# Routing weights of a mixture of experts: spread over partitions by DMA through DRAM, in place of a matmul for each block and half

## The reference

```python
hid = hidden_states + attn_out
x2 = rmsnorm(hid, ln2_w).reshape(-1, h)
probs = softmax(x2 @ gate_w.T)                        # 16 experts
top_w, top_i = top_k(probs, 4)
top_w = top_w / sum(top_w, -1)
wfull = sum(one_hot(top_i, E) * top_w[..., None], 1)  # (1024, 16)
gu = einsum('th,eih->tei', x2, w1)                    # I = 176 rows an expert
act = silu(gu[..., :I]) * gu[..., I:]
down = einsum('tei,ehi->teh', act, w2)
routed = einsum('te,teh->th', wfull, down)
shared = silu(sg) * su @ sh_down_w.T                  # 352 rows
return hid + routed + shared
```

## Time and profile before

| | |
|---|---|
| median of 3 runs | 862.36 us (861.4 to 862.72) |
| time of the profiled execution | 861.11 us |
| its span | 859.4 us |
| mean granted TensorE clock | 0.969 |
| PE, DVE, ACT, POOL busy | 769.5, 635.9, 447.4, 361.4 us |
| DMA | 28.37 MB |

### The profile page before, as it was taken

The page is one execution under the profiler, slowest core; times in us unless marked ns, Lnnn a source line. Parts: engine busy times, 40 slices in busy tenths (PEclk is TensorE's granted clock), DMA queues, the critical chain, the costliest instruction groups (busy, mean ns, idle before and its releaser), DMA issues. The chain is left out here.

```text
span 859.4 us, 12018 instructions
## 1 busy us (share of the span) xinstructions
PE 769.5 (90%) x4058; PEld 566.6 (66%) x4080; DVE 635.9 (74%) x1051; ACT 447.4 (52%) x950; POOL 361.4 (42%) x195
## 2 busy tenths in 40 slices
PE   6972887788877999999999999998689999999996
PEld 2420332334434588898889889987567888787876
DVE  5799999998998888766774776676567463736366
ACT  3557565667656356645672765466444242415141
POOL 9048999978886885111120111111253131313130
PEclk9996999989999999999999999999889999999998
DMA  8000000000000200100000010000121110202001
GB/s 297 11 1 1 0 1 0 0 1 1 0 1 1 99 1 25 50 25 26 26 26 25 24 49 25 19 20 19 55 92 56 37 57 21 71 18 73 18 0 49
DMA packets 10905, 28.37 MB, mean 33 GB/s; under 512 B 1648, under 2 KB 3184, under 8 KB 10736
## 3 DMA queue, kind: packets, MB, share of 16 engines
q1 hardware_dynamic: 10864, 27.86, 9.7%
HBM read 26.80 MB, written 1.05 MB: 32 GB/s over the span
## 5 line engine op out<-in xcount | busy, mean ns | idle before, releaser
L316 POOL TENSOR_TENSOR m_ring<-m_du,m_b_sb 128x1024 f32<-128x1024 f32 x64 | 152.5, 2402 | 26.3 <-ACT m_b_sb L549 23.8
L731 DVE TENSOR_TENSOR_SCAN m_ring<-ps,m_ring 128x1024 f32<-128x1024 f32 x64 | 145.2, 2280 | 3.5 <-ACT ps L581 3.2
L1001 POOL TENSOR_TENSOR a_wl<-raw,a_wh 128x1024 fp32r<-128x1024 f32 x16 | 39.9, 2496 | 233.3 <-ACT a_wh L1198 233.0
L425 PE MATMUL ps<-m_ring,ident 128*128 128x512 f32 x256 | 128.2, 616 | 0.4 <-DVE m_ring L736 0.4
L1489 POOL TENSOR_TENSOR e_wl<-raw,e_wh 128x512 fp32r<-128x512 f32 (+1 forms) x55 | 57.2, 1046 | 164.7 <-ACT e_wh L1605 89.8
L856 PE MATMUL ps<-e_rms_hi,e_wh 128*128 128x512 f32 x200 | 87.0, 435 | 3.6 <-ACT e_sg L1618 3.6
L581 ACT ACTIVATE ps<-m_delta,m_negA 128x510 f32<-128x510 f32 x128 | 82.6, 682 | 6.8 <-DVE ps L724 3.7
L425 PEld LDWEIGHTS ps<-m_ring,ident 128*128 128x128 f32 x256 | 50.9, 199 | 45.8 <-issue 43.1
L858 PE MATMUL ps<-e_rms_hi,e_wl 128*128 128x512 f32 x200 | 79.8, 399 | 0.0
L857 PE MATMUL ps<-e_rms_lo,e_wh 128*128 128x512 f32 x200 | 79.3, 396 | 0.0
L1618 ACT ACTIVATE e_sg<-ps 128x512 f32<-128x512 f32 x50 | 29.4, 589 | 84.3 <-PE ps L858 84.3
(11 more groups left out here) (210 smaller groups left out, 2148.8 us busy)
## 6 DMA issues: line engine op xcount, KB each, us to landing
raw<-in_expert_w SPq DMA_DIRECT2D x30, 384.0 KB, 3.0
raw<-in_attn_w SPq DMA_DIRECT2D x20, 512.0 KB, 3.3
m_first<-in_xT SPq DMA_DIRECT2D x2, 512.0 KB, 5.1
x<-in_x_tok SPq DMA_DIRECT2D x1, 1024.0 KB, 10.5
out<-hid SPq DMA_DIRECT2D x8, 128.0 KB, 2.0
m_first<-in_w_x SPq DMA_DIRECT2D x1, 512.0 KB, 7.2
m_first<-in_w_in SPq DMA_DIRECT2D x1, 512.0 KB, 8.0
raw<-in_w_out SPq DMA_DIRECT2D x1, 512.0 KB, 8.6
```

The lines of the kernel that those rows point to most:

```text
L316: nc.gpsimd.tensor_tensor(split(slot(n)), du[:, pair_of(ph):pair_of(ph) + 2, halves(ph)], b_sb[:, n % B_BUFS:n % B_BUFS + 1, :].to_broadca ...
L425: nc.tensor.matmul(ps[:, Y_BANK + c, :], ident[:, :], slot(n)[:, c * HALF:(c + 1) * HALF], start=False, stop=False, skip_group_check=True) ...
L731: nc.vector.tensor_tensor_scan(slot(n), dA_of(n), slot(n), 0.0, ALU.mult, ALU.add).then_inc(scan_done, 1)
L1001: nc.gpsimd.tensor_tensor(w[1][:, j, :], raw[:, j, :], w[0][:, j, :].bitcast(F32), ALU.subtract).then_inc(w_done, 1)
```

## The change

The weights `wf` are turned as float32 (no split in three), 16 experts on 16 partitions of PSUM banks 6 and 7, copied to `wT` (16 x 1024 float32), and stored by SP to a buffer in DRAM. From there SP loads, for each routed block, a tile `wb[:, k, :]` of 128 partitions by 1024 tokens: each partition gets the 4 KB line of its row's expert, so all partitions of one piece read the same line. A block takes two DMAs, cut where the expert changes, or in the middle. aw then multiplies by `wb` in SBUF. `u_ready` is signalled by the last up matmul. `own`, `wp` and their making fall away. SP's loop is written out; the spreads stand in one queue with the loads: first those of the two routed blocks of group 0 and of blocks 0 to 2 of group 1, then each behind a load.

```diff
@@ attention, POOL
-        nc.gpsimd.memset(own[:], 1.0).then_inc(own_ones, 1)
-        pool.wait_ge(own_ones, 1)
-        for part in range(3):
-            rows = own[NW * part:NW * (part + 1), :, :]
-            for sign, base in ((1, 0), (-1, EI - 1)):
-                nc.gpsimd.affine_select(out=rows, in_=rows, compare_op=ALU.is_ge, fill=0.0, base=base,
-                                        pattern=[[sign * P, NM_R], [sign, P]], channel_multiplier=-sign * EI
-                                        ).then_inc(own_done, 1)
-                pool.wait_ge(own_done, 2 * part + (1 if sign > 0 else 2))
@@ expert_block, SP
+            def load(g, j):
+                sp.wait_ge(w_done, g * GM + (j + 1 - GM))
+                sp.dma_start(raw[:, j, 0:FPACK], d["expert_w"][g * GM + j]).then_inc(ld_w[j], 16)
+
+            def spread(g, k):
+                row = (g * GM + k - SH_TILES) * P
+                cut = min(EI - row % EI, P)
+                cut = P // 2 if cut == P else cut
+                if g > (k < SH_TILES):
+                    sp.wait_ge(aw_done, 2 * ((g - 1) * GM + k + 1))
+                for lo, hi in ((0, cut), (cut, P)):
+                    e = (row + lo) // EI
+                    sp.dma_start(wb[lo:hi, k, :], wt_dram[e:e + 1, :].to_broadcast([hi - lo, T])
+                                 ).then_inc(ld_wb[k], 16)
+
+            for j in range(GM):
+                load(1, j)
+            sp.wait_ge(wT_done, 1)
+            sp.dma_start(wt_dram, wT[:]).then_inc(wt_stored, 16)
+            sp.wait_ge(wt_stored, 16)
+            for k in range(SH_TILES, GM):
+                spread(0, k)
+            for k in range(SH_TILES):
+                spread(1, k)
+            for g in range(2, NMG + 1):
                 for j in range(GM):
-                    sp.wait_ge(w_done, g * GM + (j + 1 - GM))
-                    sp.dma_start(raw[:, j, 0:FPACK], ...).then_inc(ld_w[j], 16)
+                    load(g, j)
+                    if g > 2 or j >= SH_TILES:
+                        spread(g - 1, j)
@@ POOL
-                if k == 0:
-                    nc.gpsimd.memset(wp[:], 0.0).then_inc(wp_clear, 1)
@@ PE, gate_up
-                    if o == 0 or shared:
-                        mm.then_inc(ready, 1)
-                if not shared:
-                    if known and n == N_SH:
-                        pe.wait_ge(wT_done, 1)
-                    pe.wait_ge(aw_done, n - 1)
-                    rows = own[:, bass.ds(g * GM + (k - SH_TILES), 1), :].rearrange("p a n -> p (a n)")
-                    nc.tensor.matmul(ps[:, 4 + th, :], rows, wT[:, toks], start=True, stop=True).then_inc(u_ready, 1)
+                    mm.then_inc(ready, 1)
@@ PE, turn_weights
-                pe.wait_ge(wp_done, 1)
-                turned = ps[:, 6, :].bitcast(BF16)
+                pe.wait_ge(wf_done, 1)
                 for i in range(TT):
-                    mm = nc.tensor.transpose(turned[:, i * P:(i + 1) * P], wp[:, i, :], identb[:])
+                    mm = nc.tensor.transpose(banks(ps, 6, 2)[0:NE, i * P:(i + 1) * P], wf[:, i, :], ident[:])
@@ DVE, routing_weights
-                chain(nc.vector.tensor_copy(wp[:, :, 0:NE], wf[:]))
-                chain(nc.vector.tensor_tensor(wr[:], wf[:], wp[:, :, 0:NE], ALU.subtract))
-                chain(nc.vector.tensor_copy(wp[:, :, NW:NW + NE], wr[:]))
-                chain(nc.vector.tensor_tensor(wr[:], wr[:], wp[:, :, NW:NW + NE], ALU.subtract))
-                nc.vector.tensor_copy(wp[:, :, 2 * NW:2 * NW + NE], wr[:]).then_inc(wp_done, 1)
@@ DVE, products
-                nc.vector.tensor_tensor(aw[:, th, :], sg[:, th, :], ps[:, 4 + th, :], ALU.mult).then_inc(aw_done, 1)
+                if th == 0:
+                    dve.wait_ge(ld_wb[k], g * 32 + 32 if k >= SH_TILES else g * 32)
+                nc.vector.tensor_tensor(aw[:, th, :], sg[:, th, :], wb[:, k, th * HALF:(th + 1) * HALF], ALU.mult
+                                        ).then_inc(aw_done, 1)
@@ DVE, tiles
-                        nc.vector.tensor_copy(wT[:], ps[:, 6, :].bitcast(BF16)).then_inc(wT_done, 1)
+                        nc.vector.tensor_copy(wT[:], banks(ps, 6, 2)[0:NE, :]).then_inc(wT_done, 1)
```

More of the change, by code:

```diff
@@ L41 @@
 NMG = NM // GM
-NW = 32
 FPACK = 3 * D
@@ L934, in attention_block @@
     hid, ident, identb, mask = (keep[k] for k in ("hid", "ident", "identb", "mask"))
-    raw, own = keep["raw"], keep["own"]
+    raw = keep["raw"]
     w, q, k_, v, p, pT, o = space.w, space.q, space.k, space.v, space.p, space.pT, space.o
@@ L940, in attention_block @@
     wh_done, w_done, hid_ready = keep["wh_done"], keep["w_done"], keep["hid_ready"]
-    own_ones, own_done = sem("own_ones"), sem("own_done")
     sq_done, root = keep["sq_done"], keep["root"]
@@ L1429, in split @@
         return sb(f"e_{name}h", shape, F32R), sb(f"e_{name}l", shape, F32R)
-    x1, hid, ident, identb, raw, own, gate_raw = (keep[k] for k in ("x1", "hid", "ident", "identb", "raw", "own", "gate"))
+    x1, hid, ident, raw, gate_raw = (keep[k] for k in ("x1", "hid", "ident", "raw", "gate"))
     ld_w = keep["ld_expert"]
@@ L1439, in expert_block @@
     wf = sb("e_wf", [P, TT, NE])
-    wr = sb("e_wr", [P, TT, NE])
-    wp = sb("e_wp", [P, TT, P], BF16)
-    wT = sb("e_wT", [P, T], BF16)
+    wT = sb("e_wT", [NE, T])
+    wb = sb("e_wb", [P, GM, T])
+    wt_dram = nc.dram_tensor("wt", (NE, T), F32, kind="Internal").ap()
     sg = sb("e_sg", [P, 2, HALF])
@@ L1454, in expert_block @@
     lg_ready, rt, ex_done = sem("lg_ready"), sem("rt"), sem("ex_done")
-    wp_clear, wp_done, wT_ready, wT_done = sem("wp_clear"), sem("wp_done"), sem("wT_ready"), sem("wT_done")
+    wf_done, wT_ready, wT_done, wt_stored = sem("wf_done"), sem("wT_ready"), sem("wT_done"), sem("wt_stored")
+    ld_wb = [sem(f"ld_wb{k}") for k in range(GM)]
     g_ready, u_ready = sem("g_ready"), sem("u_ready")
@@ L1470, in _ @@
         def _(sp):
-            with sp.Fori(1, NMG + 1) as g:
+            def load(g, j):
[21 more added lines that the diff above has]
+            for g in range(2, NMG + 1):
                 for j in range(GM):
-                    sp.wait_ge(w_done, g * GM + (j + 1 - GM))
-                    sp.dma_start(raw[:, j, 0:FPACK], d["expert_w"][bass.ds(g * GM + j, 1)].rearrange(
-                        "a p n -> (a p) n")).then_inc(ld_w[j], 16)
+                    load(g, j)
+                    if g > 2 or j >= SH_TILES:
+                        spread(g - 1, j)
             for i in range(TT):
@@ L1521, in gate_up @@
                 known = isinstance(n, int)
-                shared = known and n < N_SH
                 if th == 0:
@@ L1690, in routing_weights, with products @@
                 chain(nc.vector.reciprocal(tot[:], tot[:]))
-                chain(nc.vector.tensor_tensor(wf[:], ex[:], tot[:].to_broadcast([P, TT, NE]), ALU.mult))
-                dve.wait_ge(wp_clear, 1)
-                chain(nc.vector.tensor_copy(wp[:, :, 0:NE], wf[:]))
-                chain(nc.vector.tensor_tensor(wr[:], wf[:], wp[:, :, 0:NE], ALU.subtract))
-                chain(nc.vector.tensor_copy(wp[:, :, NW:NW + NE], wr[:]))
-                chain(nc.vector.tensor_tensor(wr[:], wr[:], wp[:, :, NW:NW + NE], ALU.subtract))
-                nc.vector.tensor_copy(wp[:, :, 2 * NW:2 * NW + NE], wr[:]).then_inc(wp_done, 1)
-            def products(n, th):
+                nc.vector.tensor_tensor(wf[:], ex[:], tot[:].to_broadcast([P, TT, NE]), ALU.mult).then_inc(wf_done, 1)
+            def products(g, k, th):
+                n = g * (2 * GM) + (2 * k + th)
                 dve.wait_ge(u_ready, n + 1)
@@ L1734, in tiles @@
                         routing_weights()
-                    products(n, 0)
+                    products(g, k, 0)
                     if k == GM - 1:
                         low(n, k, 0)
-                    products(n + 1, 1)
+                    products(g, k, 1)
                     if k < GM - 1:
@@ L1783, in constants @@
     }
-    keep["own"] = keep["rest"][:, 0:NM_R * P // 2].bitcast(BF16).rearrange("p (m n) -> p m n", n=P)
     for name in ("ld_small", "wh_done", "w_done", "hid_ready", "x_kept", "sq_done", "root"):
```

## The result

The changed kernel takes **853.78 us** (median of 4 runs, 853.27 to 855.35); the kernel before, on the same chip, 862.54 (861.4 to 863.75). The ratio is 0.9893, with a 95% interval of 0.9879 to 0.9908. The forecast was 856.8 us in a range of 852 to 861, and faster with 0.84.

What follows compares the result with a forecast made beforehand. TensorE, busy 90% of the span, was taken as the bound. Groups 1 to 4 -7.4, DRAM trip +2.1, clock +1.2 and `own` -1.5 sum to -5.6 us: 856.8 us against the runs' median of 862.36, range 852 to 861.

Steps and rivals of the forecast that it cites:

- TensorE as the clock of groups 1 to 4, 0.23 us a matmul: Expert block, groups 1 to 4: TensorE sets the time; removing forty weights' matmuls at 0.23 us each saves 9.2 us.
- The chain at a group's end, +0.45: Third `down` tile: TensorE waits for VectorE's first `add_down` behind dependent ACT and DVE steps; 0.45 us a group, 1.8 in four.
- The lock's share: Aw of half 7, both inputs now in SBUF, is held by POOL's SBUF work and loses 0.2 us a group.
- rival C: Expert block: POOL's SBUF work delays aw in every block, 0.4 x 20 = 8 us, so +2.4, 865; chance 0.05.
- Groups 1 to 4 gained 8.15, not 7.4: Expert block, groups 1 to 4: -9.2 us for removed matmuls and +1.8 for new waits, together -7.4.
- The trip through DRAM, +2.1: Group 0: storing and reloading the weights delays aw of half 6 and then the third `down` tile, +2.1 us.
- The clock, +1.2: Group 0's `down`: TensorE idle about 2.4 and 1.1 us may lower its granted clock; half of 2.4 taken, +1.2.
- case D: No clock loss and `own` counts in full: -7.2 us, 855.2, inside the range; forecast including this case has chance 0.72.
- `own`, -1.5: Attention: dropping POOL's memset and selects frees VectorE's L1319 and so TensorE; -1.5 us, bounds 0 and -1.9.
- Rival A: Group 0: the DRAM trip is hidden and all savings count, -11 to -12 us, 851; chance 0.11.
- Rival B: Spreads: the one repeated DRAM line is slow to read, making the kernel slower, +8 us, 870; chance 0.06.

Runs made afterwards that it cites:

- The kept matmul: Changed kernel with one bf16 matmul of 128 x 128 by 512 put back in each routed half, result unread: 862.21 us, ratio 0.9991.
- The two by two: Changed kernel's spreads cut by partitions or tokens, from one repeated line or different lines; the three variants: 854.71 us (partitions, different), 852.26 (tokens, repeated), 852.72 (tokens, different).
- the run of other lines: Changed kernel, but each partition's spread reads a different line from an input tensor instead of one repeated line: 854.71 us, ratio 0.99.

## Why the prediction was right

**TensorE as the clock of groups 1 to 4, 0.23 us a matmul: shown, 0.25 measured.** The kept matmul took the gain back. In group 1 of before, and then after, from the first matmul of the halves to the second of `down` are 30.04 and 27.58 us:

```profile
674.62 0.39 PE L856 MATMUL ps<-e_rms_hi,e_wh 128*128 128x512 f32 x1
...
704.66 0.28 PE L857 MATMUL ps<-e_wl,e_ah 128*128 128x256 f32 x1
```

```profile
675.60 0.39 PE L855 MATMUL ps<-e_rms_hi,e_wh 128*128 128x512 f32 x1
...
703.18 0.28 PE L856 MATMUL ps<-e_wl,e_ah 128*128 128x256 f32 x1
```

The page's busy time would have misled: PE's fell by 5.5 us only.

**The chain at a group's end, +0.45: shown.** The bracket says 0.40 in three groups and 0.28 in one. From start to start a wait costs more: in group 1 the two steps up to 707.27 began at 706.38 and took 0.89 us, where two steps take 0.23, so 0.66 was lost, of which 0.56 at the third tile itself. Moving one ScalarE operation out of the chain removed the wait. The lock's share was sized rightly. Aw of half 7 in group 1 starts 0.34 before POOL's pair ends (697.38 + 1.45 = 698.83), ends 0.54 after it, and takes 0.19 longer than 0.69; 0.2 was forecast:

```profile
697.38 1.45 POOL L1504 TENSOR_TENSOR e_wl<-raw,e_wh 128x256 fp32r<-128x256 f32 x2 [1.12 <-ACT e_wh L1609]
```

```profile
698.49 0.88 DVE L1713 TENSOR_TENSOR e_aw<-e_sg,e_wb 128x512 f32<-128x512 f32 x1
```

Over all 44 products there is little of it, which is what rival C needed much of (count: shortest, median and longest in ns):

```profile
L1713 DVE TENSOR_TENSOR e_aw<-e_sg,e_wb x44: 691/692/878, 655.6 to 830.7; 128x512 f32<-128x512 f32 x44
```

**Groups 1 to 4 gained 8.15, not 7.4.** By PE's timeline, from start to start: the halves give -9.42 where -9.2 was forecast (three groups at 27.58, one at 28.12), the waits +2.52 where 1.8 was forecast, and the steps of `down` -1.25, which no term had. So the stretch came out near its forecast in part by luck: the waits were 0.7 dearer, and the steps made up for it. These two-valued steps are told at the end; their cause is open.

**The trip through DRAM, +2.1: the mechanism as told, one term mis-sized.** In the prediction's own steps, with the block's earlier start taken off: wT was ready 0.3 us sooner than worked out; the store took 1.93 us to SP's next issue (2.1 forecast with its wake-up); **the pair landed 4.72 us after its issue, where 3.4 and 0.1 were taken**, +1.2; and from aw 6 to the third tile it was 9.68 us (9.94 forecast). Together +0.5: 2.57 in place of 2.1. The 3.4 came from one DMA of 512 KB over all partitions, and the spread is two, each over part of them. The second is issued 0.54 us after the first, where 0.1 was taken, and then moves for 4.05. The two by two shows that the shape of the pieces, and not the repeated line, makes the difference. That the whole comes within 0.5 is in part luck: in the repeat of the same kernel wT was ready 1.4 us sooner into the block (35.98 us against 37.37), and group 0 came out at 52.70, +1.54 over before. The work ahead of the turn has stretches at the lower level of the clock, and these differed (from 616 to 620 us the granted clock was 0.50, and 0.66 in the repeat).

**The clock, +1.2: too much, it was 0 in this profile and about 0.5 in the repeat.** The term was set midway between two rows, since idle times of 2.4 and 1.1 us lay between one that left the clock and one that lowered it. PE's waits came near to that, in three parts of which 0.71 was shown above:

```profile
656.92 0.51 PE L855 MATMUL ps<-e_rms_hi,e_wh 128*128 128x512 f32 x1 [0.76 <-DVE e_sg L1707]
...
662.22 0.38 PE L855 MATMUL ps<-e_wh,e_ah 128*128 128x256 f32 x1 [2.25 <-DVE e_al L1719]
```

The granted clock stayed 1.00 in every window from 650 to 670, and this execution so went by case D, which stood inside the forecast. In the repeat, waits of 0.99 and 2.23 us were followed by 0.81 and 0.85. So a loss there comes in some executions and not in others, and part of it is hidden where the slow matmuls take the place of the wait at the third tile. The term was set too large by half or more.

**`own`, -1.5: shown, and worth more than its bound of 1.9.** Of the 1.9 us of idle PE in the two windows, 1.7 was POOL's. Attention as a whole gained 2.30 in this pair of profiles; keeping `own` cost 1.9 by the medians. The table's -1.63 is near the forecast because the Mamba stage happened to end 0.67 later.

Against the sum of -5.6, the profiled runs differ by -7.5: the clock -1.2, groups 1 to 4 -0.75, the tail -0.4, the start -0.1 and the trip +0.5 make -1.95. The tail, from the third tile of group 4 to the end, was 18.55 to 18.75 us in every variant that was run and 19.02 before; why was not followed. Rival A fell: the trip was not hidden, it stayed on the path in full. Rival B fell with the run of other lines, and C with the 44 products. That the result lies above A's 851 and below the forecast's middle is not evidence for A; the missing part is the clock, the steps of `down`, and the tail. One sum of the prediction was off: halfway from -5.6 to its bounds of -9.2 and +1.2 is 1.8 down and 3.4 up, not 3 both ways; its range takes in both.

## What to carry to other kernels

Where a constant stream of matmuls sets the time, taking one out pays its step from start to start, until the next chain in line shows; look for that chain at the group's end before making the change, and for small work that stands inside it. A value that takes a way through DRAM should be worked out one block earlier than it is needed: here that was worth more (4.3 us) than a faster transfer, which brought nothing once it was done. Cut a spread by tokens over all partitions, which lands sooner (4.0 against 4.7 us or more), and keep products of two SBUF operands on VectorE out of the reach of long GpSimd work, even of work for which no one waits. And profile the same kernel twice before an effect of about 1 us in one stage is given a cause: here the second profile changed the reading of the clock and of group 0.

## What the runs showed of the hardware

Beside the rate of pieces over part of the partitions (221 to 233 GB/s against 336), two things were not expected.

The length of a wait alone does not tell whether TensorE's granted clock falls from its upper level (2.4 GHz). Waits of 0.76, 2.25 and 0.71 us, with 2.3 us of work between the last two, left it at 1.00 in the profile of the changed kernel; 0.99 and 2.23 were followed by a fall in its repeat; 3.56 us had lowered it. Near the end of attention, PE waits 0.62 and then 1.03 us in before, and 0.61 and 1.03 in the run that keeps `own`. These windows have the work behind the 1.03, before and then in that run:

```profile
592.00:596.00 4.00, 3.40 (x28) 3.27 (x29) 2.59 (x10) 2.17 (x7) 0.00 (x0) 1.00 0.00 0
```

```profile
592.00:596.00 4.00, 2.97 (x16) 2.89 (x16) 2.73 (x10) 1.91 (x9) 0.00 (x0) 0.69 0.00 0
```

What decides between the two was not found.

A matmul of 256 columns in `down` has one of two steps, which holds for at least a tile of 15. Both pairs lie at a granted clock of 1.00; the first spans 30 steps in 3.40 us (0.1133 each), in group 1, the second 30 in 3.54 (0.118), in group 2:

```profile
708.19 0.28 PE L855 MATMUL ps<-e_wh,e_ah 128*128 128x256 f32 x1
...
711.59 0.28 PE L855 MATMUL ps<-e_wh,e_ah 128*128 128x256 f32 x1
```

```profile
753.16 0.28 PE L855 MATMUL ps<-e_wh,e_ah 128*128 128x256 f32 x1
...
756.70 0.28 PE L855 MATMUL ps<-e_wh,e_ah 128*128 128x256 f32 x1
```

Over a group's 120 matmuls that would be 0.5 us. In before, group 0 had the short step and groups 1 to 4 the long one; after, only the last six tiles of group 2 and four of group 4 had the long one. That is the -1.25 us in `down` of above. The group whose halves took 28.12 us in place of 27.58 is of the same sort: its matmuls of 512 columns step by 0.2333, where the others' step by 0.229. No experiment told what chooses between them, and about 1 us of this result hangs on it.
